# A two-expert MoE layer on one core: the expert tiles, the routing steps and the weight pieces in another order

## The reference

```python
xf = einsum('bct,bcd->bdt', x, w[subjects]).reshape(4096, 512)
probs = softmax(xf @ gate_w.T); top_p, top_i = top_k(probs, 2)
out_e = (silu(xf @ fc1[e].T) * (xf @ fc2[e].T)) @ proj[e].T      # 8 experts, F = 352
shared = (silu(xf @ s1.T) * (xf @ s2.T)) @ sp.T                  # F = 1408
out = x + sum_k top_p[k] * out_e[top_i[k]] + sigmoid(xf @ sg.T) * shared
```

## Time and profile before

| | us |
|---|---|
| median of 3 runs | 1265.24 (1261.56 to 1267.28) |
| the profiled execution | 1265.67 |
| its span, first to last instruction | 1263.8 |
| PE busy | 1235.4 (98%) |
| DVE, ACT, POOL busy | 818.1 (65%), 465.7 (37%), 263.7 (21%) |

### The profile page before, as it was taken

One profiled execution on the slowest core, in us unless ns is written; L12 is line 12 of the kernel. 1 busy time (PEld: TensorE's weight loads), 2 busy tenths in 40 slices (PEclk: granted clock), 3 DMA queues, 4 the chain that ended last, 5 costly groups with the idle time before them and its releaser, 6 DMA issues.

```text
span 1263.8 us, 17260 instructions
## 1 busy us (share of the span) xinstructions
PE 1235.4 (98%) x6198; PEld 1026.2 (81%) x6198; DVE 818.1 (65%) x1330; ACT 465.7 (37%) x765; POOL 263.7 (21%) x356
## 2 busy tenths in 40 slices
PE   7999999998999999999999999999999999999998
PEld 5788888886888988888888789899787787787887
DVE  5544554458764766666665547778678778678675
ACT  4322232220111555555554456566314214213211
POOL 3267873000001121111111201110231130030110
PEclk9999999999999999999999999999999999999999
DMA  8487886202206666666664447684795875775842
GB/s 298 158 296 287 301 305 242 92 33 100 100 10 228 221 212 212 221 221 220 221 215 141 152 168 253 226 294 172 268 335 179 294 254 166 275 251 174 289 135 101
DMA packets 105411, 262.94 MB, mean 208 GB/s; under 512 B 11090, under 2 KB 11218, under 8 KB 100850
## 3 DMA queue, kind: packets, MB, share of 16 engines
q1 hardware_dynamic: 68130, 164.87, 36.9%
q0 software_dynamic: 13872, 54.27, 13.0%
q10 hardware_dynamic: 23328, 42.74, 10.3%
HBM read 195.52 MB, written 66.32 MB: 207 GB/s over the span
## 4 chain that ended last, share of the span: by engine, by line
PE 82%; DVE 10%; DMA 3%; ACT 2%; issue 1%; SPq 0%; DVEq 0%; ACTq 0%
PE bank_h L931 36%; PE bank_o L931 25%; PE bank_h L1190 8%; PE bank_t L1190 5%; PE bank_h L1072 2%; PE bank_t L910 2%; PE bank_t L931 2%; DMA x_lo<-late_up 2%; DVE h_lo L1708 1%; DVE h_sb L1704 1%; DVE w_lo L1825 1%; PE bank_t L860 1%; DVE h_hi L1706 1%; PE bank_o L870 1%; ACT g_sb L1385 1%
## 5 line engine op out<-in xcount | busy, mean ns | idle before, releaser
L931 PE MATMUL bank_h<-x_hi,w_hi 128*128 128x512 f32 (+1 forms) x768 | 279.5, 364 | 4.3 <-DVE h_sb L1704 4.3
L931 PE MATMUL bank_h<-x_hi,w_lo 128*128 128x512 f32 (+1 forms) x768 | 272.7, 355 | 0.0
L931 PE MATMUL bank_h<-x_lo,w_hi 128*128 128x512 f32 (+1 forms) x768 | 272.6, 355 | 0.0
L818 POOL DMA_INDIRECT rows<-xf_rows,token_of x71 | 69.0, 972 | 578.6 <-PE bank_t L910 393.4
L931 PE MATMUL bank_o<-wp_hi,h_hi 128*128 128x512 f32 (+1 forms) x442 | 181.2, 410 | 2.8 <-DVE h_lo L1708 2.8
L931 PE MATMUL bank_o<-wp_lo,h_hi 128*128 128x512 f32 (+1 forms) x442 | 177.6, 402 | 0.0
L931 PE MATMUL bank_o<-wp_hi,h_lo 128*128 128x512 f32 (+1 forms) x442 | 177.2, 401 | 0.0
L931 PEld LDWEIGHTS bank_h<-x_hi,w_hi 128*128 128x128 f32 x768 | 145.9, 190 | 23.4 <-DVE h_sb L1704 5.2
L931 PEld LDWEIGHTS bank_h<-x_hi,w_lo 128*128 128x128 f32 x768 | 145.5, 189 | 20.8
L931 PEld LDWEIGHTS bank_h<-x_lo,w_hi 128*128 128x128 f32 x768 | 146.0, 190 | 17.7
L1825 DVE TENSOR_TENSOR w_lo<-raw,w_hi 128x640 fp32r<-128x640 f32 (+1 forms) x116 | 92.3, 834 | 40.6 <-ACT w_hi L1252 40.6
(11 more groups left out here) (266 smaller groups left out, 2315.2 us busy)
## 6 DMA issues: line engine op xcount, KB each, us to landing
raw<-ew SPq DMA_DIRECT2D x29, 1408.0 KB, 6.5
w_early<-late_up ACTq DMA_DIRECT2D x69, 256.0 KB, 4.1
slot_rows<-res SPq DMA_DIRECT2D x32, 512.0 KB, 3.1
rawp<-ewp SPq DMA_DIRECT2D x29, 512.0 KB, 7.2
x_hi<-late_up ACTq DMA_DIRECT2D x46, 256.0 KB, 3.9
x_lo<-late_up ACTq DMA_DIRECT2D x46, 256.0 KB, 2.8
xt_in<-xf_transposed SPq DMA_DIRECT2D x11, 1024.0 KB, 7.2
late_up<-raw POOLq DMA_DIRECT2D x6, 1792.0 KB, 7.6
```

The lines of the kernel that those rows point to most:

```text
L818: pool.indirect_dma_start(rows[:, row % 4, :], None, xf_dram, bass.IndirectOffsetOnAxis(token_of[:, HALF_OF[row]:HALF_OF[row] + 1].bitcast ...
L931: mm = pe.matmul(dst, a, m, start=(first and i == 0), stop=(last and i == 2))
```

## The change

It reorders; no arithmetic is added or removed. The tiles become ten `W`, seven pairs `SQ`, `QQQ`, `WW`. Of the routing, `route_weights` and the first part of `expert_starts` go between the output rows of block 4, the rest of it (now `expert_tiles`) and `slot_bases` stay behind them; `choice_slots` is cut into `choice_offsets` (its first ten operations) and the rest, which is joined with `slot_places`; `tile_experts` goes from behind block 5's last hidden to behind its second output row. The transposed rows begin at fixed places 0, 4, 11, 15 and 22 of the down products. Weight piece 3 goes behind the second hidden of a tile and DVE's piece 5 behind the third; in the pairs pieces 4 and 5 go before the Q's third hidden. The first block's late x is loaded in one go after tile 23. A Q's third chunk uses `maps` as scratch in place of `picked`, into which that x is loaded.

```diff
-KINDS = "WW" + "SQ" * SINGLES + "Q" * (QUADS - SINGLES) + "W" * TAIL
+KINDS = "W" * TAIL + "SQ" * SINGLES + "Q" * (QUADS - SINGLES) + "WW"
...
+PLAIN = TAIL + 2 * SINGLES
...
         def u_folded(i):
-            return picked_flat[:, 0:BN] if KINDS[i] == "Q" else h_sb[:, 3 * TS:4 * TS]
+            return maps[:, :, :].rearrange("p s d -> p (s d)") if KINDS[i] == "Q" else h_sb[:, 3 * TS:4 * TS]
...
             while i < XT - 2:
-                if i == XT - 7:
-                    sp.wait_ge(shared[0].x_lo, BLOCKS - 1)
...
-                if i - 1 in (XT - 6, XT - 5):
-                    load_late_x(0, i - 1 - XT + 6)
+                if i == PLAIN:
+                    sp.wait_ge(shared[0].x_lo, BLOCKS - 1)
+                    for t in range(2):
+                        load_late_x(0, t)
...
-            def turning(order):
+            def turning(order, starts=(0, 4, 11, 15, 22)):
-                todo = [(row, k) for row in order for k in range(KC)]
+                todo = {at + k: (row, k) for row, at in zip(order, starts) for k in range(KC)}
+                slots = [0]
                 def small(i=0):
-                    if todo:
-                        row, k = todo.pop(0)
+                    if slots[0] in todo:
+                        row, k = todo.pop(slots[0])
                         transpose_row(row, (k,))
+                    slots[0] += 1
...
             def tile_step(i, first=False):
-                last = KINDS[i + 1] == "S"
-                for at in range(3):
-                    if first:
+                if first:
+                    expert_gate(i, 0)
+                w_waits(i + 1)
+                for at, pieces in enumerate(((0, 1), (2,), (3, 4, 5))):
+                    if first and at:
                         expert_gate(i, at)
-                    if at == 0:
-                        w_waits(i + 1)
-                    split_w(i + 1, (i + 1) % 2, (2 * at, 2 * at + 1))
+                    split_w(i + 1, (i + 1) % 2, pieces)
...
                 split_w(i + 2, 1 - u, (0, 1))
                 expert_gate(i + 1, 1)
-                split_w(i + 2, 1 - u, (2, 3))
+                split_w(i + 2, 1 - u, range(2, 6))
                 expert_gate(i + 1, 2)
-                split_w(i + 2, 1 - u, (4, 5))
...
-            shared_tail(0, FULL + 1)
-            route_weights()
-            expert_starts()
+            shared_tail(0, FULL + 1, between=steps_of({0: route_weights, 2: expert_starts}))
+            expert_tiles()
             slot_bases()
-            hiddens(0, FULL + 2, between=steps_of({0: choice_slots, 1: slot_places, 2: lambda: choice_ids(0),
-                                                   3: lambda: choice_ids(1), 4: tile_experts}))
-            shared_tail(0, FULL + 2)
+            hiddens(0, FULL + 2, between=steps_of({0: choice_offsets, 1: choice_slots, 2: lambda: choice_ids(0),
+                                                   3: lambda: choice_ids(1)}))
+            shared_tail(0, FULL + 2, between=steps_of({1: tile_experts}))
...
             def tile_step(i, first=False):
                 u, single = (i + 1) % 2, KINDS[i + 1] == "S"
-                for at in range(3):
+                for at, pieces in enumerate(((0, 1), (2,), (3, 4))):
                     if first:
                         expert_hidden(i, at)
-                    split_w(i + 1, u, (2 * at, 2 * at + 1), single)
+                    split_w(i + 1, u, pieces, single)
                     if not first:
                         expert_hidden(i, at)
+                split_w(i + 1, u, (5,))
...
                 expert_hidden(i + 1, 1)
-                split_w(i + 2, 1 - u, (2, 3), single)
+                split_w(i + 2, 1 - u, range(2, 6), single)
                 expert_hidden(i + 1, 2)
                 for row in turned_early(i + 1):
                     rest_row(row)
-                split_w(i + 2, 1 - u, range(KC, PIECES))
+                split_w(i + 2, 1 - u, (6,))
...
+            for i in range(XT - 1):
+                if KINDS[i] == "S":
+                    single_and_quad(i)
+                elif not (i and KINDS[i - 1] == "S"):
+                    tile_step(i, i == 0)
+                if i in (PLAIN + 1, PLAIN + 2, XT - 2):
+                    late_sum(0, {PLAIN + 1: 0, PLAIN + 2: 1, XT - 2: 2}[i])
```

More of the change, by code:

```diff
@@ L1416, in single_and_quad @@
                 split_w(i + 1, u, range(2, PIECES))
-                act.wait_ge(single_turned, i // 2)
+                act.wait_ge(single_turned, KINDS[:i + 1].count("S"))
                 for j in (slice(0, 2), slice(2, 3)):
@@ L1598, in expert_starts, with expert_tiles @@
                                                   op0=ALU.add, op1=ALU.add))
+            def expert_tiles():
                 ends = scan[:, :, TILES - 1:TILES].rearrange("p e t -> p (e t)")
@@ L1655, in tile_experts, with choice_offsets @@
                 link(nc.vector.tensor_copy(tile_expert[:, :], te_f))
-            def choice_slots():
+            def choice_offsets():
                 link(nc.vector.tensor_tensor(scan[:, :, :], scan[:, :, :], total[:, :, :], ALU.subtract))
@@ L1667, in choice_slots @@
                 link(nc.vector.tensor_tensor(total, total, rest, ALU.add))
+            def choice_slots():
                 for k, mask in enumerate((top1, top2)):
@@ L1670, in choice_slots @@
                     link(nc.vector.tensor_reduce(posf[:, k * TILES:(k + 1) * TILES], over_e(tmp[:, :, :]), AX_X, ALU.add))
-            def slot_places():
                 slots = slot_of[:, :, :].rearrange("p k t -> p (k t)")
@@ L1745, in row_sum, with shared_tail @@
                                                in1=res[:, r, :], op0=ALU.mult, op1=ALU.add).then_inc(f.o_kept, 1)
-            def shared_tail(n, b, front=0):
+            def shared_tail(n, b, front=0, between=None):
                 if n == 0 and not (isinstance(b, int) and b > FULL + 1):
@@ L1757, in shared_tail @@
                         rest_xt(n, b + 1)
+                    if between:
+                        between(r)
             def steps_of(at):
@@ L1893, in _ @@
             split_w(0, 0, range(KC, PIECES))
[L1894 to L1898, removed]
             def late_sum(b, q):
```

## The result

The changed kernel takes 1250.98 us (median of four runs, 1250.27 to 1251.41) where the kernel before takes 1264.26 beside it (1261.56 to 1267.28): the ratio is 0.9894, 95% interval 0.987 to 0.9918. The forecast was 1252.5, the range 1247.9 to 1258.6. The profiled execution took 1250.27, with a span of 1248.4.

What follows compares the result with a forecast made beforehand. PE was taken to bound the kernel, so only its stops could give time: routing 5.6, transposed rows 4.1 and W tiles 3.3 make 13.0, from 1265.67 or the median 1265.24, forecast 1252.5, range 1247.9 to 1258.6.

Steps and rivals of the forecast that it cites:

- Routing: Blocks 4 to 6: the new step order removes stops and slow clock worth 6.2, less a new 0.6, gaining 5.6.
- The new stop at the fifth hidden: Block 5's first output row: PE waits for the fifth hidden, between 0 and 0.9, taken as 0.6.
- The clock: After the routing's stop of 2.8: slow matmuls lose 1.6; the other stop, 1.5, left none.
- Transposed rows: Waits at a Q's third row: nine stops vanish at the new places, 4.1 gained, ends 0 and 4.6.
- The fifth row ends six places later: End of a Q tile: the row and POOL's gather come 1.4 later, wanted only by the next tile.
- tenth stop: Transposed rows: ten Qs but nine stops listed, the view supposedly leaving one out; 0.5 in the range.
- W tiles: First down product of nine W's: waits vanish as hiddens come earlier, 3.3 gained, ends 0 and 3.4.
- Piece 5 now stands ahead of the rows: DVE in the W tiles: this piece takes 0.65 and brings the rows back to where they were.
- the 0.2 to spare: A Q's third row: PE arrives 0.68 later at a wait of 0.48, if DVE is not later.
- Rival (b): Transposed rows: the wait only moves, all 4.1 stays, time 1256.6; chance 0.12.
- At nothing: Tile order, late x load, SP's moved wait, DVE's three sums and scratch address: priced at no time.
- rival (d): Expert stage start: ten W's outrun their weights, PE stops, time 1271.6 and more; chance 0.05.

Runs made afterwards that it cites:

- e1: The kernel before with the new order of the routing steps alone; 1257.47 us, ratio 0.9956.
- e10: The changed kernel with the routing steps in the order of the kernel before; 1256.31 us, ratio 0.9946.
- e11: The changed kernel again, without an edit; 1251.31 us, ratio 0.9904.
- e7: The changed kernel with the last tile's second hidden ahead of the late x and block 5's second ids behind its fifth hidden; 1249.72 us, ratio 0.9894.
- e2: The kernel before with the new places of the transposed rows, and the pairs' pieces ahead of the last hidden; 1260.25 us, ratio 0.9976.
- e3: The kernel before with the new weight piece places in the W and plain Q tiles alone; 1260.28 us, ratio 0.9977.
- e4: The kernel before with the new tile order alone, and the late x load and scratch that go with it; 1264.63 us, ratio 1.0007.
- e9: The changed kernel with block 5's own routing steps as they were, so half of the new routing order; 1250.94 us.
- e5: The changed kernel with the plain Q tiles' weight pieces back at their old places; 1251.81 us, ratio 0.9912.
- e12: The changed kernel with the five mends of four single-mend runs together; 1247.31 us, ratio 0.9872.
- e6: The changed kernel with a Q's fifth row transposed two places earlier and a W's three rows in one run; 1251.17 us, ratio 0.9904.
- e8: The changed kernel with the single tile's hidden transposed one product (three matmuls) later; 1250.25 us, ratio 0.9901.

## Why the prediction was right, point by point

**The bound.** PE paces the kernel, and time came only from its stops: right. No other stage moved, but for the late one, which varies without the change too.

**Routing, 5.6 forecast.** Block 5 gave 5.9 in the profiles, e1 5.8 in its runs, and e10 against e11 5.0. The chain came out link by link. Less the 0.8 by which block 5 starts later in the changed profile, the first hidden began at 292.5 (293.26; forecast 292.5), the second at 298.8 (299.64; 298.9), and the fifth ended at 314.9 (313.86 to 315.72; 315.0). The new stop at the fifth hidden was expected at 0.6 and measured 0.37 + 0.11 (the first matmul behind it), and its cause is shown: with the ids moved (e7) it is gone.

**The clock.** I priced 1.6 for it in the stop of 2.8 and nothing in one of 1.5. All five profiles with the stop of 2.8 (before, e2, e3, e4, e10) have 48.4 to 48.5 in block 5, and from 303 to 311 their granted clock is 0.79 to 0.81 in the mean; in e9, with one stop of 1.4, it stays at the upper level. The times and clocks of all runs show more: of the 29 runs of the kernel before, 8 have a granted clock of 1.0 over the whole kernel, with a mean of 1262.0, and 21 have 0.997 to 0.999, with a mean of 1264.0; of the 40 runs of kernels without that stop (changed, e1, e5 to e9, e11, e12) 39 have 1.0, and of the 41 that keep it (e2, e3, e4, e10) 5. So the same stop seems to lower the clock in most executions and not in all; which stretch fell in a run without a profile isn't shown, and the profile of e4 has a second fall, in the front stage (0.91 from 20 to 40). No run has the stop of 2.8 without the one of 1.5 ahead of it, so whether the 2.8 alone would do it isn't shown either. What the Trainium skill says in "TensorE: Matmul & The Clock Gate", Part 1, that the chip's watch over activity runs free of the program, fits these 8 and 21, which don't prove it.

**Transposed rows, 4.1 forecast.** Alone they gave 3.5 in the tiles and 3.0 in the runs. The step that the stops go at the new places was right in the pairs (0.44 each for 0.48). Two things were left out. "The fifth row ends six places later, and POOL's gather behind it by as much, 1.4; its row is wanted by the next tile" looked at POOL and not at ACT, where the split of that row stands ahead of the copies that free the banks of the next single tile: 0.19 at each S, of which 0.13 shows (e6). And the W ahead of the first pair turns three rows, the third of which moved from place 8 to 11: that made the first single tile 0.4 longer, once. One reading was wrong: the view leaves no tenth stop out. The tenth Q stands ahead of a W and turns two rows, so it has no third row to wait for; it takes 24.59 before and in e2, and the 0.5 that the range has for it stands on nothing.

**W tiles, 3.3 forecast.** Each W gained 0.44 for 0.37 (e3), as the first matmul behind a stop is slow as well. But the working costed the W's alone, and the edit serves the plain Qs too. There "Piece 5 now stands ahead of the rows, 0.65, which brings them back to where they were" holds only where DVE comes to the third hidden without idling. In a plain Q it idles ahead of it for the gate (1.89 in e3), so the piece came on top, and the row that PE waits for came later by it: the 0.2 to spare was gone, and the three plain Qs gained nothing in the whole (79.25 for 79.28), where the rows alone would have given 0.9 (e5). This is the failed step. Rival (b), that the wait at the rows stays, came true at two of the nine places.

**Tiles in sum.** 7.4 was forecast (4.1 + 3.3), 6.6 measured. With routing, 13.0 against 12.5: the routing's excess of 0.3 covers part of the tiles' loss of 0.8, and that is luck.

**At nothing.** The order: 0.3 in the tiles, nothing in the runs (e4). W's ahead did not outrun their weights: from the third tile to the tenth they follow one another every 13.24, and the list of waits has none of PE in the first ten, so rival (d) had no part. The last tile's stop stayed, 0.93 idle, as forecast; e7 shows that the order of the late x around it was its cause.

**The sum against the median.** I took 13.0 from an execution of 1265.67. Its late stage was 3 longer than in most of the other profiles, so the 1250.98 of the median lies below my 1252.5 not because a term of the change was larger.

## What to carry to other kernels

When an edit sits in a shared function, cost it for every kind of tile that calls it, with the slack of each: here the same line gave 0.44 to each W and cost each of two Qs 0.6 (e3). When a step moves later on one engine, follow every engine that reads it to what stands behind it there, down to the copies that free a bank. And cut the profiles into stages at fixed starts of the pacing engine before comparing them: gains of 0.4 in a part are plain there, while the runs differ by 2 for reasons that are not the change's.

## What the runs showed that I had not expected

The late stage, with the same code in each but for the order of the late x in e7 and e12, took 368.5 to 372.3 in fourteen profiles; part of it is the waits for its weights, 2.6 in the kernel before's waits by name and 0.2 in the changed kernel's. What sets them was not found. A W takes 13.20 in some profiles (e3, e5, e6, e7, e9) and 13.24 in others (changed, e8, e10, e11, e12), without a stop in either; this too stays open.

A wait of 0.1 to 0.2 can be absent from the list of waits and show only as a start that comes late: 0.35 for 0.23 at 580.83.
